# The routing table of two mixture-of-experts layers: one-hot rows in 16 bits with another axis innermost, and a shared marking pass

## What is computed

```python
probs = jax.nn.softmax(x @ gate_w + gate_b, axis=-1)
topk_probs, topk_idx = jax.lax.top_k(probs, TOP_K)            # TOP_K = 2
cw = jnp.sum(jax.nn.one_hot(topk_idx, N_EXPERTS, dtype=x.dtype) * topk_probs[..., None], axis=2)
...
x = x + 0.5 * _L1_ffn_ref(_layernorm(x, axis=-1), ...)        # expert layer 1
x = x + _L1_attn_ref(_layernorm(x, axis=-1), ...)
x = x + 0.5 * _L1_ffn_ref(_layernorm(x, axis=-1), ...)        # expert layer 2
```

## Time and profile before

| | us |
|---|---|
| median of three runs | 2328.38 |
| the profiled execution, its own time | 2326.32 |
| its span in the trace | 2324.6 |
| VectorE / GpSimd / ScalarE / TensorE busy | 1764.5 / 907.5 / 958.9 / 1960.7 |
| first table, from the first `hot_hi` to the copy of the bank | 859.56 to 883.07 |
| second table, the same | 1995.90 to 2019.42 |

### The profile page before, as it was taken

How to read it: one execution, slowest core, us unless ns; L and a number is a source line. 1 busy time by engine, 2 the same in 40 slices (tenths; PEclk the granted TensorE clock), 3 DMA queues, 4 the chain that set the end, 5 groups by cost and what they waited for, 6 DMA issues and landing times. The chain is left out here.

```text
span 2324.6 us, 36254 instructions
## 1 busy us (share of the span) xinstructions
PE 1960.7 (84%) x11363; PEld 1301.0 (56%) x11363; DVE 1764.5 (76%) x3598; ACT 958.9 (41%) x1892; POOL 907.5 (39%) x910
## 2 busy tenths in 40 slices
PE   2899997889999747989978599999999995398998
PEld 1566665756666426877866233333333363287787
DVE  7798874578887667877978577777777646687788
ACT  1222223322222443433557255555555537143345
POOL 2444442134444467887245300000000026588853
PEclk9999997989999858999989699999999996599999
DMA  5000000100000342223526534334334006222246
GB/s 177 1 0 0 0 0 14 42 0 1 0 0 0 97 159 64 92 87 101 170 69 168 98 55 70 51 54 69 50 55 70 2 1 195 75 89 89 89 148 191
DMA packets 116655, 156.59 MB, mean 67 GB/s; under 512 B 20966, under 2 KB 85772, under 8 KB 115980
## 3 DMA queue, kind: packets, MB, share of 16 engines
q1 hardware_dynamic: 99840, 112.83, 20.9%
q0 software_dynamic: 14400, 40.41, 5.6%
q10 hardware_dynamic: 2252, 1.29, 0.2%
HBM read 107.00 MB, written 47.20 MB: 66 GB/s over the span
## 5 line engine op out<-in xcount | busy, mean ns | idle before, releaser
L2021 DVE TENSOR_REDUCE t_nm<-ps 128x1 f32<-128x512 f32 (+3 forms) x768 | 390.9, 553 | 106.3 <-PE ps L2111 53.5
L2087 ACT ACTIVATE t_E<-ps 128x1024 f32<-128x1024 f32 (+3 forms) x384 | 295.0, 808 | 248.0 <-PE ps L2139 194.9
L1507 PE MATMUL ps<-m_w,m_xT 128*128 (+1 forms) x1248 | 347.1, 414 | 0.8 <-DVE m_xT L1587 0.8
L1507 PEld LDWEIGHTS ps<-m_w,m_xT 128*128 128x128 f32 x1248 | 222.5, 191 | 38.2 <-issue 1.4
L567 POOL TENSOR_TENSOR f_h<-f_h,f_hmagic 128x704 f32<-128x704 f32 x64 | 108.1, 1689 | 293.4 <-DVE f_h L209 293.4
L605 PE MATMUL ps<-wgT,f_xT 128*128 128x352 f32 x512 | 187.8, 516 | 38.5 <-DVE f_h L523 36.4
L2006 POOL COPY t_Va<-t_V 128x128 f32<-128x128 f32 x64 | 16.1, 295 | 491.7 <-DVE t_mp L2032 491.5
L2136 PE MATMUL ps<-t_Qs,t_Ks 98*128 98x512 bf16 (+3 forms) x768 | 199.8, 341 | 6.0 <-DMA t_Qs<-t_mT 4.1
L1525 PE MATMUL ps<-m_w,m_hT 128*128 (+1 forms) x1248 | 199.7, 296 | 0.5 <-DVE m_hT L1604 0.5
L639 PE MATMUL ps<-wdT,f_hT 128*128 128x256 f32 (+1 forms) x768 | 189.5, 389 | 7.4 <-DVE X L557 5.4
L1559 ACT ACTIVATE m_hT<-ps 128x256 fp32r<-128x256 f32 x208 | 80.1, 385 | 227.9 <-PE ps L1516 226.7
(11 more groups left out here) (296 smaller groups left out, 3950.0 us busy)
## 6 DMA issues: line engine op xcount, KB each, us to landing
m_raw<-in_L_ffn_rw SPq DMA_DIRECT2D x48, 256.0 KB, 3.3
t_parts<-t_qkv_part SPq DMA_DIRECT2D x64, 192.0 KB, 2.8
t_Qs<-t_parts SPq DMA_DIRECT2D x96, 128.0 KB, 4.0
t_Ks<-t_parts SPq DMA_DIRECT2D x96, 128.0 KB, 6.6
m_yl<-m_picked_out SPq DMA_DIRECT2D x40, 256.0 KB, 3.2
m_rows<-m_xn SPq DMA_DIRECT2D x16, 512.0 KB, 4.3
m_xg<-m_rows SPq DMA_DIRECT2D x64, 128.0 KB, 2.8
m_y<-m_picked_out SPq DMA_DIRECT2D x24, 256.0 KB, 3.3
```

What stands on the lines that cost most here:

```text
L1507: last = nc.tensor.matmul(ps[:, H1 + u, :], xT[:, u, kx, k, :], of_expert(w1, kw, e, k), start=n == 0, stop=n == 3 * DC - 1)
L2021: nc.vector.tensor_reduce(dst, ps[:, bank, 0:n], AX_X, ALU.max, negate=True).then_inc(emptied, 1)
L2087: nc.scalar.activation(E[:, s % NPB, :, 0:n], ps[:, bank:bank + 2, 0:n], ACT.Exp, scale=float(HD) ** -0.5).then_inc(e_ok, 1)
```

## The change

The one-hot rows get another order of axes and other input types. `hot_lo` and `hot_hi` now have the chunk's picks column innermost ([128][8] and [72][8] in a partition, before [8][128] and [8][72]). The count comes from `count_up`, a bf16 copy of the count with each number eight times, and the places from `places`, a bf16 copy of `place[:, 1:3]`. So both comparisons have only 16-bit operands with step one innermost. `marked` keeps its order, so that a picks column's 144 columns lie together for TensorE; each marking pass therefore reads along the picks columns and writes with a step of 144 elements (288 bytes). TensorE's weight `hot_lo[:, k % 2, :, j]` is now read with a step of 8 elements (16 bytes).

The marking by the picks column's number stays on GpSimd in chunks 0, 2, 4 and 6; in chunks 1, 3, 5 and 7 VectorE does it after its two comparisons, with a drain ahead, from the bf16 list `picks`. ScalarE makes `count_up` (1024 elements) and `picks` (64) once per table, after the exponential and ahead of its last four weight pieces, behind a wait for the stores of `xn`. The name `hots(k)` counts VectorE's increments of `hot_ok` ahead of chunk k.

```diff
--- before.py
+++ after.py
@@ -976,9 +976,12 @@
                 xT = ch.sb(name + "xT", [P, 2, 2, DC, GN], F32R, ctx=rctx)
             with ExitStack() as rctx:
                 pr = ch.sb(name + "pr", [P, 4, TILES, EXPERTS], ctx=rctx)
-                hot_lo = ch.sb(name + "hot_lo", [P, 2, CH, P], BF16, ctx=rctx)
-                hot_hi = ch.sb(name + "hot_hi", [P, 2, CH, NT], BF16, ctx=rctx)
+                hot_lo = ch.sb(name + "hot_lo", [P, 2, P, CH], BF16, ctx=rctx)
+                hot_hi = ch.sb(name + "hot_hi", [P, 2, NT, CH], BF16, ctx=rctx)
                 marked = ch.sb(name + "marked", [P, 2, CH, 2, NT], BF16, ctx=rctx)
+                picks = ch.sb(name + "picks", [P, PICKS], BF16, ctx=rctx)
+                count_up = ch.sb(name + "count_up", [P, P, CH], BF16, ctx=rctx)
+                places = ch.sb(name + "places", [P, 2, PICKS], BF16, ctx=rctx)
                 over = ch.sb(name + "over", [P, NT, EXPERTS], ctx=rctx)
                 table = ch.sb(name + "table", [P, 4, NT], ctx=rctx)
             stats, rstd_ok, xn_ok, x_turned, x_high, x_stored, logit_ok, shifted, exp_ok = map(
@@ -986,6 +989,12 @@
             w_high, w_split, loaded_b, router_ok = map(sem, ("w_high", "w_split", "loaded_b", "router_split"))
             taken_ok, counted, placed, hot_ok, row_ok, pick_ok, tabled = map(
                 sem, ("taken", "counted", "placed", "hot", "row_marked", "pick_marked", "tabled"))
+            count_ok = sem("count_up")
+
+            def hots(k):
+
+                return 2 * k + k // 2
+
             raw_in = [sem(f"raw_in{k}") for k in range(RAW)]
             xn_out = [sem(f"xn_out{k}") for k in range(2)]
             rows_ok, rows_out = sem("logit_rows"), sem("logit_rows_out")
@@ -1159,15 +1168,22 @@
                     nc.vector.scalar_tensor_tensor(out=place[:, 2, :], in0=place[:, 1, :], scalar=-float(P),
                                                    in1=place[:, 0, :], op0=ALU.mult, op1=ALU.add).then_inc(placed, 1)
                     drain()
+                    nc.vector.tensor_copy(places[:, :, :], place[:, 1:3, :])
+                    drain()
+                    dve.wait_ge(count_ok, 1)
 
                     for k in range(PICKS // CH):
                         cols = slice(k * CH, (k + 1) * CH)
                         if k >= 2:
                             dve.wait_ge(tabled, k - 1)
-                        tt(hot_hi[:, k % 2, :, :], ch.iota[:, 0:NT].unsqueeze(1).broadcast_to([P, CH, NT]),
-                           place[:, 1, cols].unsqueeze(2).broadcast_to([P, CH, NT]), ALU.is_equal).then_inc(hot_ok, 1)
-                        tt(hot_lo[:, k % 2, :, :], ch.iota[:, :].unsqueeze(1).broadcast_to([P, CH, P]),
-                           place[:, 2, cols].unsqueeze(2).broadcast_to([P, CH, P]), ALU.is_equal).then_inc(hot_ok, 1)
+                        tt(hot_hi[:, k % 2, :, :], count_up[:, 0:NT, :],
+                           places[:, 0, cols].unsqueeze(1).broadcast_to([P, NT, CH]), ALU.is_equal).then_inc(hot_ok, 1)
+                        tt(hot_lo[:, k % 2, :, :], count_up[:, :, :],
+                           places[:, 1, cols].unsqueeze(1).broadcast_to([P, P, CH]), ALU.is_equal).then_inc(hot_ok, 1)
+                        if k % 2:
+                            drain()
+                            tt(marked[:, k % 2, :, 0, :].rearrange("p c n -> p n c"), hot_hi[:, k % 2, :, :],
+                               picks[:, cols].unsqueeze(1).broadcast_to([P, NT, CH]), ALU.mult).then_inc(hot_ok, 1)
                     dve.wait_ge(tabled, PICKS // CH)
                     got = [table[:, k, :] for k in range(4)]
                     nc.vector.tensor_copy(table[:, 0:2, :], ps[:, TABLE, 0:2 * NT].rearrange("p (k n) -> p k n", k=2))
@@ -1219,13 +1235,13 @@
                             low_piece(k)
                     for k in range(2 * GROUPS, PIECES):
                         low_piece(k)
-                    for k in range(PICKS // CH):
-                        pool.wait_ge(hot_ok, 2 * k + 1)
+                    for k in range(0, PICKS // CH, 2):
+                        pool.wait_ge(hot_ok, hots(k) + 1)
                         if k >= 2:
                             pool.wait_ge(tabled, k - 1)
                         nc.gpsimd.tensor_tensor(
-                            marked[:, k % 2, :, 0, :], hot_hi[:, k % 2, :, :],
-                            ch.iota[:, k * CH + 1:(k + 1) * CH + 1].unsqueeze(2).broadcast_to([P, CH, NT]), ALU.mult
+                            marked[:, k % 2, :, 0, :].rearrange("p c n -> p n c"), hot_hi[:, k % 2, :, :],
+                            ch.iota[:, k * CH + 1:(k + 1) * CH + 1].unsqueeze(1).broadcast_to([P, NT, CH]), ALU.mult
                         ).then_inc(pick_ok, 1)
 
                 @block.tensor
@@ -1285,12 +1301,13 @@
                                             taken[:, :, :].rearrange("p j e -> p (j e)"), start=False, stop=True)
                     last.then_inc(counted, 1)
                     for k in range(PICKS // CH):
-                        pe.wait_ge(hot_ok, 2 * k + 2)
+                        pe.wait_ge(hot_ok, hots(k + 1))
                         pe.wait_ge(row_ok, k + 1)
-                        pe.wait_ge(pick_ok, k + 1)
+                        if k % 2 == 0:
+                            pe.wait_ge(pick_ok, k // 2 + 1)
                         for j in range(CH):
                             n = k * CH + j
-                            last = nc.tensor.matmul(ps[:, TABLE, 0:2 * NT], hot_lo[:, k % 2, j, :],
+                            last = nc.tensor.matmul(ps[:, TABLE, 0:2 * NT], hot_lo[:, k % 2, :, j],
                                                     marked[:, k % 2, j, :, :].rearrange("p t n -> p (t n)"),
                                                     start=n == 0, stop=n == PICKS - 1)
                         last.then_inc(tabled, 1)
@@ -1342,13 +1359,18 @@
                         high_piece(k)
                     act.wait_ge(shifted, 1)
                     nc.scalar.activation(pr[:, 0, :, :], pr[:, 0, :, :], ACT.Exp).then_inc(exp_ok, 1)
+                    for k in range(2):
+                        act.wait_ge(xn_out[k], 16 * GROUPS // 2)
+                    nc.scalar.activation(count_up[:, :, :], ch.iota[:, :].unsqueeze(2).broadcast_to([P, P, CH]), ACT.Copy
+                                         )
+                    nc.scalar.activation(picks[:, :], ch.iota[:, 1:PICKS + 1], ACT.Copy).then_inc(count_ok, 1)
                     for k in range(PIECES - 4, PIECES):
                         high_piece(k)
                     for k in range(PICKS // CH):
-                        act.wait_ge(hot_ok, 2 * k + 1)
+                        act.wait_ge(hot_ok, hots(k) + 1)
                         if k >= 2:
                             act.wait_ge(tabled, k - 1)
-                        nc.scalar.activation(marked[:, k % 2, :, 1, :], hot_hi[:, k % 2, :, :], ACT.Copy,
+                        nc.scalar.activation(marked[:, k % 2, :, 1, :].rearrange("p c n -> p n c"), hot_hi[:, k % 2, :, :], ACT.Copy,
                                              scale=ch.row1[:, 0:1]).then_inc(row_ok, 1)
 
         xg = ch.sb(name + "xg", [P, RING, D], ctx=ctx)
```

## The result

The changed kernel takes 2334.22 us, the median of 20 runs (2326.43 to 2346.55); the kernel before, over 20 runs of the same comparison, 2325.99 us. The ratio is 1.0037, with a 95% interval of 1.0023 to 1.0052: slower by 8.2 us between the medians and 8.6 by the ratio, where 8.7 us faster was forecast.

The account below looks back on a forecast made before the run. VectorE and GpSimd taking turns were held to bound two table stretches on the path. Pairs of chunks at 1.98 + 1.20 + 1.20 = 4.38 us make a table 19.17 against 23.51, saving 8.7 in all: 2319.7 us, range 2311 to 2330.

Parts of the forecast that it names:

- The comparisons: VectorE's two one-hot passes per chunk: doubled pace with 16-bit operands, `hot_hi` 0.76 to 0.46 us, `hot_lo` 1.21 to 0.68.
- The sum: Two chunks of the table loop on VectorE's clock: 1.98 + b + x = 4.38 us, before 5.52.
- b and x: b: GpSimd's marking body, behind `hot_lo`'s end; x: VectorE's new marking pass; each taken as 1.20 us.
- upper bound of 2.07: Most that either marking pass was thought to take, in us: GpSimd's whole pass in the kernel before.
- The lock: GpSimd's passes and VectorE's two-input SBUF passes take turns; a held `hot_hi` ends 0.31 us after GpSimd's body.
- P: Time of two chunks in the table loop, 1.98 + b + x, forecast 4.38 us; a table has four such pairs.
- ScalarE's marks: ScalarE's marking pass per chunk, 0.78 us: ends before the others' marks, even if the step doubles it.
- Copies, cast, weight loads: ScalarE's two copies, 1.4 to 1.5 us, hidden; cast with drain 0.27 us; TensorE's stepped weight loads no slower.
- The rival on the other side: A pair's marking passes become the bound from b + x = 3.49; at 2.07 each, 2333.6 us; chance 0.14.
- 13.94 - 4(b + x): Microseconds saved per table as a function of both marking prices; 4.34 at the forecast's 1.20 each.
- both bounds: Both marking passes, GpSimd's and VectorE's, at 2.07 us each.
- no doubled pace: Rival: VectorE's comparisons stay at 0.76 and 1.21 us; each table loses 2.22 us, 2332.8 in all; chance 0.10.

Follow-up runs that it names:

- the dense version: Changed kernel, but all three marking passes read with a 16-byte step and write neighbours; 2311.45 us, ratio 0.9938 to the kernel before; again on another chip, 0.9953.
- the sweep: Changed kernel plus, behind each table, the marking pass alone on VectorE, ScalarE, GpSimd at eight write steps and one stepped read; VectorE 0.46 us dense, 2.56 to 2.71 hopping.

## Why the prediction was wrong, point by point

- **Where and what: right.** The change lies in two stretches on the path, and the tables' 2 x 4.4 us account for the change of the whole.
- **The comparisons: right.** 0.46 and 0.68 us forecast, 0.46 and 0.68 measured.
- **The sum: right.** With the dense version's measured marks, 1.27 and 1.17, it gives 4.42 us for two chunks, and 4.42 were measured. The mechanism holds; what failed is a price put into it.
- **The step that failed: the price of the marks, b and x.** The forecast took b = 1.20 and x = 1.20, "nearer to the row of the same engine". Measured: b = 2.49 and x = 2.59, both above the upper bound of 2.07. That bound was GpSimd's whole pass, which contained some 0.8 us of holding and no write with a hop, so it was no bound for one. The reason given against dear marks, that it would take over twice the time per element on both engines, is what happened: the sweep has VectorE's pass at 0.46 us dense and 2.56 with the hop, and the dense version has the whole loss back. The Trainium skill's page that spoke against the change (Vector Engine (DVE) Microarchitecture Reference, 5.2) pointed the right way, but by its price, x up to 1.6 us, the change would still have paid. The Trainium skill has there, for 4-byte words, 1.73 ns per column where one source hops 4 KiB with every element, and 1.71 to 2.50 where the output hops. Here, with 2-byte elements and 0.16 us taken off as what the dense pass needs beyond 576 x 0.52 ns, the stepped read has (1.17 - 0.16) / 576 = 1.75 ns, which agrees. The hopping write has (2.58 - 0.16) / 576 = 4.2 ns, and the measurement decides for that larger price. Whether the 2-byte elements make the difference, no run shows.
- **The lock: right, with a different end.** `hot_hi` was held as said. But in the changed kernel it ended at 858.77, 0.17 us before GpSimd's pass (858.94), where the sum had 0.31 after; with dense marks it was 0.32 after. VectorE's next `hot_hi` also started 0.35 us before the end of its slow mark (861.70, and 859.47 + 2.58), not 0.08; it took 0.64 for 0.46, so 0.09 of that was gained. The forecast's own P with the measured b and x, 1.98 + 2.49 + 2.59, gives 7.06; less 0.48 and 0.09 that is 6.49, and 6.54 were measured.
- **ScalarE's marks: right by luck.** "If the step doubles them, still" covered 1.6 us; they took 2.78. They still ended before the others' (861.59 and 862.05 in the second chunk), but only since those had become so dear: with the others dense this alone gives a table of 22.0 us.
- **Copies, cast, weight loads: right.** 1.04 and 0.24 us for the two copies, hidden: GpSimd's 13 subtractions took 17.10 us, before 17.17. The cast's stretch is 0.30 for 0.27. A chunk's weight loads with a 16-byte step take 0.91 us, before 0.85, and its matmuls 1.16, before 1.12. The Trainium skill (SBUF — State Buffer, Specifications, on cachelines) has a penalty for accesses that each cross to a new 16-byte line, without a size. On the weight side it is 0.06 us a chunk here, on the moving side 1.0 (2.17 against 1.16).
- **The rival on the other side was the right one**: the marks as the bound, from b + x = 3.49 on. Its place and mechanism were as it said; its price, 2.07 each, was too low, and so was its chance of 0.14. The measured loss in the tables, 8.8 us, lies beyond the 5.2 that its bounds gave, and the median above the range's 2330. By 13.94 - 4(b + x) the measured prices would even lose 6.4 us a table; the earlier ends, told under the lock, made it 4.4. (With both bounds and no doubled pace the text on record has a loss of 9.1 per table; its own sum gives 9.2.)

## What to carry to other kernels

When a layout is turned so that one pass gets neighbours, find the pass that loses them, and price it as a write that leaves its neighbour with every element: here 4.2 ns an element on VectorE, against 0.52 for the same pass written densely. If the transposition can't be avoided, let the pass read with the step and write densely (1.17 us against 2.59 for the same 576 elements). And a row is an upper bound only for what it contains: the 2.07 us that bounded the marks contained holding, and no write with a hop.

## What was not expected of the hardware

- Three engines whose dense passes take 0.46, 0.77 and 1.29 us all take 2.56 to 2.85 with a hopping 2-byte write, at each of five distances from 144 to 576 bytes.
- A stepped write is dear well before it hops: 8 bytes apart, 1.44 us against 0.46 on VectorE; a read 16 bytes apart, only 1.17.
- TensorE's two inputs differ: eight weights read with a step of 16 bytes take 0.91 us against 0.85, eight matmuls that read their moving columns so 2.17 against 1.16, at the lower clock.
- By its times a held VectorE pass is let in before GpSimd's has ended. Taken at their unheld lengths, the held passes began 0.15 us before GpSimd's end in the kernel before (863.08 - 0.76, against 862.47) and 0.14 with dense marks (854.46 - 0.46, against 854.14), but 0.63 where GpSimd's write hops (858.77 - 0.46, against 858.94).
